# Slot layer of a decoder block: a narrower alpha, an output product in two row groups, and a new order on every engine

## The reference

```python
ctx = jnp.concatenate([x, jnp.broadcast_to(slot_mean, x.shape)], axis=-1)
h = jax.nn.gelu(ctx @ w1.T + b1, approximate=False)
route_logits = (h @ w2.T + b2) / (jnp.abs(tau) + 0.1)
topk_vals, topk_idx = jax.lax.top_k(route_logits, TOP_K)
topk_w = jax.nn.softmax(topk_vals, axis=-1)
alpha = jnp.sum(topk_w[..., None] * jax.nn.one_hot(topk_idx, Sn, dtype=x.dtype), axis=-2)
slot_input = jnp.einsum('bts,btd->bsd', alpha, x)
gi = slot_input / (alpha.sum(axis=1) + 1e-08)[..., None]
gx, gh = gi @ gru_wih.T + gru_bih, hs @ gru_whh.T + gru_bhh     # hs: the slots, the same for every sequence
r, z = sigmoid(xr + hr), sigmoid(xz + hz)
n = jnp.tanh(xn + r * hn)
slot_values = ((1.0 - z) * n + z * hs) @ wv.T + bv
out = jnp.einsum('bts,bsd->btd', alpha, slot_values) @ wo.T + bo
```

## Time and profile before

| | before |
|---|---|
| median of 3 runs | 1803.64 us (1802.96 to 1803.95) |
| profiled execution | 1802.11 us |
| its span, first to last instruction | 1800.4 us |
| mean granted TensorE clock | 0.974 |
| busy over the span | PE 91%, DVE 76%, ACT 54%, POOL 52% |

### The profile page before, as it was taken

The page is one execution under the profiler, slowest core; times in us unless marked ns, Lnnn a source line. Parts: engine busy times, 40 slices in busy tenths (PEclk is TensorE's granted clock), DMA queues, the critical chain, the costliest instruction groups (busy, mean ns, idle before and its releaser), DMA issues. The chain is left out here.

```text
span 1800.4 us, 51162 instructions
## 1 busy us (share of the span) xinstructions
PE 1635.2 (91%) x17566; PEld 1172.6 (65%) x17566; DVE 1372.7 (76%) x3280; ACT 974.4 (54%) x2049; POOL 942.0 (52%) x1202
## 2 busy tenths in 40 slices
PE   2799999999999999998799999999999946999997
PEld 1566666666666666665477777777777733666664
DVE  4698998898989898897366766666666634899896
ACT  1355555555455555554365555555656522777774
POOL 2355545554555545554346666666666660545544
PEclk9899999999999999999899999999999976999999
DMA  5555445554555445543000000000000001000001
GB/s 101 81 86 92 82 83 83 88 87 82 83 84 91 82 79 88 86 79 59 24 14 20 12 17 12 17 12 17 12 17 13 6 25 54 25 30 32 32 29 41
DMA packets 124322, 92.63 MB, mean 51 GB/s; under 512 B 34849, under 2 KB 122850, under 8 KB 124258
## 3 DMA queue, kind: packets, MB, share of 16 engines
q1 hardware_dynamic: 124258, 91.80, 28.1%
HBM read 23.06 MB, written 8.39 MB: 17 GB/s over the span
## 5 line engine op out<-in xcount | busy, mean ns | idle before, releaser
L1158 POOL TENSOR_SCALAR_AFFINE_SELECT probs_t<-probs_t 128x512 f32<-128x512 f32 x256 | 185.6, 739 | 218.7 <-ACT probs_t L847 218.4
L1620 DVE TENSOR_REDUCE c_neg_max<-score_banks 128x16 f32<-128x2048 f32 x64 | 146.6, 2291 | 179.8 <-PE score_banks L1401 179.8
L1729 POOL TENSOR_SCALAR_AFFINE_SELECT c_probs_t<-c_probs_t 128x512 f32<-128x512 f32 x256 | 154.9, 639 | 12.8 <-ACT c_probs_t L1549 12.8
L1549 ACT ACTIVATE c_probs_t<-score_banks 128x512 f32<-128x512 f32 x256 | 131.8, 601 | 32.8 <-PE score_banks L1427 32.8
L517 PE MATMUL score_banks<-xn_t,w_qk_a 128*128 128x256 f32 x512 | 133.0, 394 | 0.7 <-ACT xn_t L756 0.7
L1740 POOL TENSOR_TENSOR c_scaled<-c_normed,gamma 128x512 f32<-128x512 f32 x32 | 40.6, 1269 | 138.9 <-DVE c_normed L1603 138.9
L1424 PE MATMUL score_banks<-c_q_f,c_k_z 32*128 32x128 f32 x2048 | 105.7, 305 | 6.9 <-DVE c_neg_max L1620 2.3
L666 PE MATMUL bank<-probs_t,v_heads 128*32 128x128 f32 x2048 | 109.0, 285 | 2.5 <-POOL probs_t L1158 0.7
L1424 PEld LDWEIGHTS score_banks<-c_q_f,c_k_z 32*128 32x128 f32 x2048 | 91.5, 187 | 26.7 <-DVE c_neg_max L1620 17.4
L995 DVE TENSOR_REDUCE neg_max<-score_banks 128x4 f32<-128x512 f32 x128 | 87.6, 684 | 18.7 <-PE score_banks L578 18.6
L517 PEld LDWEIGHTS score_banks<-xn_t,w_qk_a 128*128 128x128 f32 x512 | 91.2, 193 | 9.9 <-ACT xn_t L756 1.1
(11 more groups left out here) (266 smaller groups left out, 4689.2 us busy)
## 6 DMA issues: line engine op xcount, KB each, us to landing
q_stack<-qk_part SPq DMA_DIRECT2D x192, 128.0 KB, 3.5
k_stack<-qk_part SPq DMA_DIRECT2D x192, 128.0 KB, 4.6
c_ctx_in<-in_ctx SPq DMA_DIRECT2D x32, 256.0 KB, 2.7
out<-y SPq DMA_DIRECT2D x32, 256.0 KB, 2.1
x_sb<-in_x SPq DMA_DIRECT2D x30, 256.0 KB, 2.7
rq_stack<-lat_part SPq DMA_DIRECT2D x192, 32.0 KB, 2.4
rk_stack<-lat_part SPq DMA_DIRECT2D x192, 16.0 KB, 1.9
w_ih<-in_ffn_w_ih SPq DMA_DIRECT2D x1, 768.0 KB, 4.7
```

What stands on the lines that cost most here:

```text
L1158: nc.gpsimd.affine_select(out=pt[:], in_=pt[:], pattern=[[0, 4], [1, 128]], compare_op=ALU.is_ge, fill=0.0, base=-1 if local else 0, chann ...
L1549: nc.scalar.activation(probs_t[tt][:, 4 * g:4 * g + 4, :].rearrange("p j q -> p (j q)"), score_banks[:, g, :], ACT.Exp, scale=SCALE).then_ ...
L1620: nc.vector.tensor_reduce(neg_max[:, tt, :], all_scores, AX.X, ALU.max, negate=True).then_inc(max_done, 1)
L1729: nc.gpsimd.affine_select(out=heads, in_=heads, pattern=[[0, 4], [1, 128]], compare_op=ALU.is_ge, fill=0.0, base=0, channel_multiplier=-1) ...
```

## The change

- `alpha` is 64 columns for each sequence, without zeros. Both halves together are one 128 x 128 tile, and one transpose gives `alpha_t` of 128 x 128: slots of the first sequence on partitions 0 to 63, of the second on 64 to 127. It goes into the bank of the `gi` transposes (columns 256 to 383) and is issued behind them; `transpose_alpha` and its semaphore are gone.
- The output product of each sequence multiplies its own 64 rows (`alpha_t[half]` and `slot_val[half]`) and writes a bank of its own (`bank[2:4]`) instead of half a bank. `y` reads both banks with one instruction of the same 128 x 512 elements.
- `b_vo` is gone: since the weights of a token sum to one, the value bias goes into the output bias once, as `b_all`, which `f_x_bias` adds. `slot_val` becomes a plain copy from PSUM, on ScalarE instead of VectorE.
- The logits share the bank of the hidden product (columns 256 to 383), so `hidden` also waits for the `logits` of the pair before.
- The order of the operations in a step is new on TensorE, ScalarE and VectorE. GpSimd's is the same. On VectorE, `rz` belongs to pair k-3 now and is the first of its step. The wait of `top` for `logits` now stands in an instruction of its own that also counts up a semaphore, `dve_turn`, for which nobody waits.

The diff's core. The tiles, the biases and the banks:

```diff
-    alpha_all = sb("alpha", [128, 2, 2, PS])
-    alpha = [alpha_all[:, i, :, :] for i in range(2)]
-    alpha_t = [sb(f"alpha_t{i}", [128, 2, 128]) for i in range(4)]
+    alpha = [sb(f"alpha{i}", [128, 2, SLOTS]) for i in range(2)]
+    alpha_t = [sb(f"alpha_t{i}", [128, 128]) for i in range(4)]
...
-            nc.vector.memset(alpha_all[:], 0.0).then_inc(prep_v, 1)
...
-            nc.vector.tensor_copy(b_vo[:], bank[6][:, 0:D]).then_inc(prep_v, 1)
+            nc.vector.tensor_tensor(b_all[:], bank[6][:, 0:D], b_o[:], ALU.add).then_inc(prep_v, 1)
...
-    tr_bank, hid_bank, logit_bank, in_bank, gate_bank, new_bank, out_bank = (
-        bank[0], bank[1], bank[2], bank[3], bank[4:6], bank[6], bank[7])
+    tr_bank, hid_bank, out_bank, gate_bank, new_bank, in_bank = (
+        bank[0], bank[1], bank[2:4], bank[4:6], bank[6], bank[7])
+    logit_bank = hid_bank[:, PT:PT + 2 * SLOTS]
```

TensorE, the output product and the order of a step:

```diff
                 for tt in range(2):
-                    mm = pe.matmul(out_bank[:, D * tt:D * tt + D], alpha_t[at.off % BY][:, tt, :], slot_val[:],
+                    half = slice(SLOTS * tt, SLOTS * tt + SLOTS)
+                    mm = pe.matmul(out_bank[tt][:, 0:D], alpha_t[at.off % BY][half, :], slot_val[half, :],
...
-                for back, what in ((2, slot_inputs), (1, route), (0, transpose_x), (4, transpose_slots),
-                                   (2, transpose_alpha), (2, transpose_inputs), (0, hidden), (4, slot_values),
-                                   (2, gates), (4, give_out)):
+                for back, what in ((4, transpose_slots), (1, route), (0, transpose_x), (2, slot_inputs),
+                                   (4, slot_values), (0, hidden), (2, transpose_inputs), (4, give_out), (2, gates)):
```

ScalarE, the moved operation and the order of a step:

```diff
+            def slot_values(at):
+                act.wait_ge(val_filled, at.count(1, 1))
+                wait(act, out_filled, at.count(1, 0))
+                nc.scalar.activation(slot_val[:], new_bank[:, 0:D], ACT.Copy).then_inc(val_ready, 1)
...
-                for back, what in ((3, gates), (0, copy_xn), (4, copy_slots), (2, copy_alpha),
-                                   (2, copy_inputs), (3, candidate), (1, exp), (0, gelu)):
+                for back, what in ((4, copy_slots), (3, gates), (0, copy_xn), (1, exp), (4, slot_values),
+                                   (3, candidate), (2, copy_inputs), (2, copy_alpha), (0, gelu)):
```

VectorE, the order of a step:

```diff
-                if fed.real:
-                    mean_inputs(fed)
+                if updated.real:
+                    gates(updated)
                 if routed.real:
                     route_logits(routed)
                 if norms:
                     norm_moments()
+                if routed.real:
+                    dve.wait_ge(logit_ready, routed.count(1, 1))
+                    dve.sem_inc(dve_turn, 1)
+                    route_top(routed)
+                    route_mark(routed)
+                if fed.real:
+                    mean_inputs(fed)
                 if updated.real:
                     candidate(updated)
-                if routed.real:
-                    dve.wait_ge(logit_ready, routed.count(1, 1))
                 if at.real and second.real:
                     dve.wait_ge(ln_step, following.count(2, 2))
                     norm_stats(second)
-                if routed.real:
-                    route_top(routed)
-                    route_mark(routed)
-                if given.real:
-                    slot_values(given)
                 if norms:
                     norm_scale(following)
+                if routed.real:
+                    route_weights(routed)
                 if updated.real:
                     new_slots(updated)
-                if routed.real:
-                    route_weights(routed)
-                if fed.real:
-                    gates(fed)
                 if given.real:
                     output(given)
```

More of the change, by code:

```diff
@@ L1803, in slots @@
     w_vo = sb("w_vo", [128, C, D])
-    b_vo = sb("b_vo", [128, D])
+    b_all = sb("b_all", [128, D])
     stats = sb("f_stats", [128, 2, 6])
@@ L1971, in slot_inputs @@
                 wait(pe, giT_ready, at.count(1, 0))
+                wait(pe, alphaT_ready, at.count(1, 0))
                 for tt in range(2):
                     half = slice(SLOTS * tt, SLOTS * tt + SLOTS)
[L1974 removed]
+                    mm = pe.matmul(in_bank[half, 0:XW], alpha[at.par][:, tt, :], xn[at.off % BY][:, tt, :],
                                    start=True, stop=True, skip_group_check=True)
@@ L2013, in slot_values @@
                 mm.then_inc(val_filled, 1)
-            def transpose_alpha(at):
-                wait(pe, y_ready, at.count(1, -2))
-                for tt in range(2):
-                    mm = pe.transpose(out_bank[:, 128 * tt:128 * tt + 128], alpha[at.par][:, tt, :], ident[:])
-                mm.then_inc(alphaT_filled, 1)
             def transpose_inputs(at):
```

53 lines of the change are left out of this document (25 added, 28 removed).

## The result

The changed kernel takes **1812.45 us** (median of 5 runs, 1811.73 to 1814.22), the kernel before in the same sitting 1803.64 (5 runs, 1802.93 to 1805.0): ratio 1.0050, 95% interval 1.0037 to 1.0064. It is slower, by 8.8 us where 20 were forecast.

What follows compares the result with a forecast made beforehand. The VectorE–GpSimd loop of 8.32 us a step was taken as the bound; 19 steps at +0.81, 7 at +0.55 and 1 us for the rest gave +20 us on 1802.1 + 1.5: 1824 us, range 1797 to 1833.

Steps and rivals of the forecast that it cites:

- What bounds the kernel before: Slot stage: loop from rz through r_hn_c (3.00 us) and VectorE's run from n_in to rz (5.32) makes the 8.32 us step.
- The walk up to h_n: New step timed from rz: neg_top stalls 0.57 to 0.60 us beside r_hn, costing 0.25; h_n starts at 4.82.
- the price of a wait behind logits: VectorE, top's separate wait with increment: 0.03 to 0.10 us, so neg_top starts at 1.42 to 1.46 against r_hn at 1.43.
- the wait of chosen: VectorE's chosen pair: the first stalls 0.53 us beside h_n, the second 1.08 beside f_x_bias.
- The premise: GpSimd gets in between two contending VectorE instructions in a row, as with the c_xn pair, 1.73 us in all.
- number 3: chosen doesn't stretch and slips past; z_hn meets the last 0.5 us of f_x_bias: 7.8 us a step, 1790 us; chance 0.06.
- The sign named for this case: Profile after: chosen staying at 0.22 us means phase or rule is wrong, steps 7.6 to 7.9 us, set by TensorE's gates.
- rival 1: neg_top goes ahead of r_hn in every step, leaving only chosen's stalls, 0.55 us a step: 1819 us; chance 0.27.
- rival 5: The change does nothing: gains and stalls cancel, with chosen stalled once in two steps: 1803 us; chance 0.04.
- Every fourth step lets neg_top come first: Steps turning the hardware loop have later r_hn, so neg_top doesn't stall: 7 steps lose 0.55 us, the other 19 lose 0.81.
- three quarters: TensorE's busy share in the slot stage after the change, down from 46.5 of 50 us, with its waits on VectorE.
- The data paths: alpha without zeros and 64-row output product: savings off the loop, worth 0; b_all takes slot_val's 0.33 us off VectorE.

Runs made afterwards that it cites:

- e9: Kernel before the change, with f_x_bias cut to 8 of 256 columns in its old place: 1794.00 us, ratio 0.9939 to the kernel before.
- e3: Changed kernel with top in a PSUM bank instead of SBUF: 1806.07 us, ratio 1.0012 to the kernel before.
- e5: Changed kernel with one spare VectorE max between the second f_xn and the first chosen: 1826.15 us, ratio 1.0114 to the kernel before.
- e11: Changed kernel with f_x_bias heading GpSimd's step, top in PSUM, and route_weights (chosen to alpha) ahead of f_xn: 1784.13 us, ratio 0.9889 to the kernel before.
- e4: Changed kernel's data paths with the old order on TensorE, ScalarE and VectorE: 1803.50 us, ratio 0.9996 to the kernel before.
- e10: New data paths in the old order, with f_x_bias cut to 8 of 256 columns: 1798.45 us, ratio 0.9970 to the kernel before.
- e12: New data paths in the old order, f_x_bias cut to 8 columns, ScalarE's exp ahead of slot_val: 1792.15 us, ratio 0.9927 to the kernel before.
- e6: Changed kernel with a spare GpSimd memset and a wait for it between h_n and f_x_bias: 1811.28 us, ratio 1.0032 to the kernel before.
- e1: Changed kernel with f_x_bias moved to the head of GpSimd's step: 1797.30 us, ratio 0.9959 to the kernel before.
- e8: Kernel before the change, with only f_x_bias moved to the head of GpSimd's step: 1830.63 us, ratio 1.0139 to the kernel before.
- e7: Changed kernel with f_x_bias at the head of GpSimd's step and top in a PSUM bank: 1789.19 us, ratio 0.9912 to the kernel before.

## Why the prediction was right in direction and wrong in size

- **What bounds the kernel before** held: e9 shows the pair f_xn's 0.32 us on VectorE's loop, and n_in's wait for r_hn_c is gone after the change.
- **The walk up to h_n** held closely: n_in was put at 3.25 us after rz and came at 3.27, chosen at 4.90 and came at 4.89, h_n at 4.82 and came at 4.82. neg_top loses to r_hn, by 0.05 us, in nearly all steps (median 0.69 us in 32), and e3 shows what it costs. One term of it stands on thin ground: top was put at 1.05 to 1.09 by the price of a wait behind logits. It came at 1.10, just as the two f_moments ended (1612.86 and 0.24 us), which stand between and which the walk left out. So the outcome came as forecast, but no run shows the price of that wait.
- **The step that failed** is the wait of chosen: "Now the first waits for h_n ... and the second comes ... 0.06 after f_x_bias, and waits for it". h_n was issued 0.07 us ahead of chosen, as forecast, and still stood back for both. With no stall on chosen, alpha comes as f_x_bias starts, and takes the stall in its place: one of 1.05 us instead of two of together 1.61. That is 8.56 against the forecast's 9.13 us, some 0.56 a step. The premise, that between two such VectorE instructions in a row GpSimd gets in, rested on one pair. By the walk's own times h_n (4.82) is issued while the second f_xn runs (4.58 to 4.98), and in this branch the walk didn't ask who goes next when it ends. With one instruction put between, chosen does wait and the step is 9.14 (e5), so the other terms of the loop's step were sound. Why h_n stands back for chosen stays open.
- **A second chance was missed**: of the rivals, number 3 came nearest (chosen doesn't stretch, the next victim is met by f_x_bias), but it put the victim at z_hn with 0.5 us left of f_x_bias and the step at 7.8. It took chosen to be immune; in e5 it is not. The sign named for this case (chosen at 0.22, so steps of 7.6 to 7.9) failed with it: chosen is at 0.22 and the step at 8.57.
- **The range was right by luck.** 1812.45 lies in 1797 to 1833, but no branch had it: the forecast's own range began at 1820, rival 1 stood at 1819 and rival 5 at 1803.
- **"Every fourth step lets neg_top come first"** did not happen: neg_top loses in all steps of the loop, and one in four takes 8.62 us. What was missed is that one in four takes 8.56 us, not 8.32, in the kernel before and so loses 0.02, some 1.2 us less in all than at 0.25 a step; and that the four steps ahead of the loop run in a worse phase, 9.0 us each, some 1.7 us more. The two nearly cancel, by luck. In e5 too the fourth steps cost close to the forecast's 0.55 by luck: they take 9.14 like the others, against 8.56 before.
- **TensorE** was to be busy three quarters of the time; the row says 45.66 of 50, which is 7.8 us of a step of 8.59, what it was before. The three quarters were a slip of mine: 7.8 of the forecast's own 9.13 is 0.85. The bound of 7.6 us by TensorE proved about right: e11 waits for it at 7.75 us a step.
- **The data paths** were taken to cost nothing, and the 0.33 us of slot_val was counted as a gain on VectorE within the new order. In the old order it brought nothing at all (e4), for reasons that no term of the sum had (e10, e12).
- The Trainium skill, page SBUF — State Buffer, section Who interferes with whom, says that issue order decides who blocks. e5, the first four steps and z_hn in e6 agree; the step shown above doesn't, since h_n was issued first and was itself held, by 0.29 us. It also says that an instruction with at most one SBUF input, outside the two-port modes, doesn't contend: e3 agrees for an input in PSUM, 0.16 us beside r_hn.

## What to carry to other kernels

When instructions of two engines hold each other up, write down for each long instruction of one the first contending instruction of the other that it can meet, and the next one if it slips: removing a stall mostly hands it on, and work taken off the waiting engine is given back as a longer wait for the same end. Move the long instruction to where nothing contends, and ask of every move what it waits for there and who stands behind it in its queue (e1 against e8: the same edit, -6.7 and +24.7 us). Before an order is judged, find the bound below its stalls; here, with two collisions gone that were decided by 0.02 and 0.05 us, the same order on TensorE, ScalarE and VectorE is 16.7 us faster than the kernel before (e7).
